# 8-wide attentions of a four-layer block: softmax division moved from the probabilities to the outputs

## The chip, the cores and the metric

The kernel runs on one core of a Trainium2 chip. The metric is the device time of one execution in microseconds. Before the change three runs took 3652.41, 3653.56 and 3655.22 us; the median is 3653.56 us.

## The reference

The program computes four layers one after the other on x of shape (16, 256, 128), float32: each adds an attention and a feed-forward part of the normalised x to x. The change touches the attentions of the first two layers, which have 16 heads of width 8:

```python
# layer 0 (layer 1 has biases, its own rope, and no mask)
q, k, v = heads(x @ Wq.T), heads(x @ Wk.T), heads(x @ Wv.T)     # (b, 16, 256, 8)
q, k = rope(q), rope(k)
scores = einsum('bhqd,bhkd->bhqk', q, k) * SCALE + causal_mask
attn = softmax(scores, axis=-1)
out = einsum('bhqk,bhkd->bhqd', attn, v)
return out.transpose(0, 2, 1, 3).reshape(b, n, 128) @ Wo.T + bo
```

## The kernel before

`program` normalises x (`norm_tiles`), then calls `prepare8` (line 274: turned and rotated weights) and `attention8` (line 319) for layer 0, with the int8 feed-forward of that layer (`Int8`) interleaved ahead of its loop; then it normalises again and calls `attention8` for layer 1. Everything else of the program (the ternary feed-forward, chunked attention, routed experts, slot experts, iterated attention) is outside of the change.

There is no planner: each engine has a program of its own, written out by hand as a loop, and engines meet through counting semaphores (`c.steps`). `attention8` works in B = 16 batches of 256 tokens. A batch is eight pairs of heads (PB = 8), so that p runs over 128 pairs, and a step j = p % 8. The steps of a pair:

- PE, `scores(p)` (line 380): two blocks of 128 queries for each of two heads, 32 rows of the array each, into PSUM banks 0 to 3, alternating; in layer 0 the causal mask is added by four bf16 matmuls. It waits for the exps of pair p-2, and at j = 0 for `laid`, the batch's queries and keys in place.
- DVE, `maxima` (line 488): a row maximum for each head over 128x512, negated.
- ACT, `exps` (line 562): two exps of 128x256 a head, which also accumulate the row sums into `rsum` (the accumulator is read out by an instruction of its own).
- DVE, `invert` (line 496): the reciprocal of the row sums. POOL, `norm` (line 609): probabilities times reciprocal, 128x512 a head.
- PE, `turn` (line 402), two pairs later: four transposes a head. ACT `move_even` (line 573) and DVE `move_odd` (line 502) copy them to SBUF.
- PE, `weigh` (line 412), after every second pair: sixteen matmuls for four heads, with the values as stationary operand, 32 columns a head. Within the 32 rows of a head r = h % 4 the eight values of head h stand at column 8 * (h // 4), zeros elsewhere (`lay_v`, line 475), so that the four groups of a batch accumulate in one PSUM tile O of 128x256. The order of the features is then a permuted one, for which `prepare8` permutes Wo by `perm`.
- Once a batch: ACT `copy_out` (line 579), PE `through_wo` (line 370), DVE `add` (line 508).

The queries and keys of a batch are prepared beside this: PE `project(b, j)` (line 351; j = 0 the queries, 1 the keys; `w[k]` and the rotated `w[k + "r"]`), DVE `rope_turn` (line 456), POOL `rotate` (line 603), DVE `hi_lo` (line 467: a rounded part and the rest), then SP (line 630) writes both parts to DRAM (`spilled`, line 640) and, after both have landed there, reads them back in another layout (`spread`, line 651; two DMAs of 256 KB). ACT `lay` (line 556) casts the landed 128x1024 into `q` or `k` and signals `laid`. All of SP's DMAs are in one queue in program order: batch by batch, queries, then keys. The loop has the keys of batch b+1 projected at step 0 of batch b and the queries of batch b+2 at step 6; `lay` of batch b+1 stands at steps 2 and 5 on ACT.

Of the kernel before, what the change touches and what calls it, by code (L numbers as in the profile page):

```python
# [16 lines left out]
P = 128  # L17
# [26 lines left out]
def const_columns():  # L44
# [9 lines left out]
    f = np.arange(P)  # L54
    head, d = f // HD8, f % HD8
    perm = np.zeros((P, P))
    perm[f, 32 * (head % 4) + HD8 * (head // 4) + d] = 1.0
    c["perm"] = perm
# [196 lines left out]
class Tiles8:  # L255


    def __init__(self, nc, sb):
# [8 lines left out]
        self.nm, self.rsum, self.rinv = (sb(f"a8_{k}", [P, 4, 2, TB]) for k in ("nm", "rsum", "rinv"))  # L267
# [3 lines left out]
        self.wo = [sb(f"a8_wo{i}", [P, D]) for i in range(2)]  # L271


def prepare8(c, t, w0, w1, bias1, perm):
# [4 lines left out]
    made, kept, zeroed = c.steps("w_made", 2), c.steps("w_kept", 2), c.steps("v_zeroed", 2)  # L279
# [3 lines left out]
    def pe_program():  # L283
# [7 lines left out]
        for n, k in enumerate("qk"):  # L291
            pe.matmul(c.banks[6][:, n * D:(n + 1) * D], t.tmp[:, n, :], c.turn, start=True, stop=True)
            pe.matmul(c.banks[6][:, 2 * D + n:2 * D + n + 1], c.turn, bias1[k], start=True, stop=True)
        pe.matmul(c.banks[7][:, 0:D], perm, t.w0[:, 3, :], start=True, stop=True)
        pe.matmul(c.banks[7][:, D:2 * D], perm, w1["o"], start=True, stop=True).then_inc(made.sem, 1)

    def act_program():
# [6 lines left out]
        act.copy(t.br1[:, :], c.banks[6][:, 2 * D:2 * D + 2])  # L304
        for i in range(2):
            ins = act.copy(t.wo[i][:, :], c.banks[7][:, i * D:(i + 1) * D])
        ins.then_inc(kept.sem, 1)
# [8 lines left out]
    return kept.all(), zeroed.all()  # L316


def attention8(c, x, xnT, tiles, ready, w, wo, rope, bias, causal, beside=None):
    nc = c.nc  # L320
    pe, act, dve, pool, sp = nc.tensor, nc.scalar, nc.vector, nc.gpsimd, nc.sync
    O, M = c.banks[6][:, 0:N], c.banks[7]
# [6 lines left out]
    t1, t2, rot, Pr, PTs, oT = tiles.t1, tiles.t2, tiles.rot, tiles.Pr, tiles.PTs, tiles.oT  # L329
    nm, rsum, rinv = tiles.nm, tiles.rsum, tiles.rinv  # L330
# [9 lines left out]
    scored, weighed = c.steps("scored", NP), c.steps("weighed", NP // 2)  # L340
    maxed, exped, inverted, normed, turned = (c.steps(k, 2 * NP) for k in ("maxed", "exped", "inverted", "normed", "turned"))
    even, odd = c.steps("even_moved", NP), c.steps("odd_moved", NP)
    out_moved, through, added = c.steps("out_moved", B), c.steps("through_wo", B), c.steps("added", B)

    def pe_program():
# [24 lines left out]
        def through_wo(b):  # L370
            if b + 2 < B:
                pe.wait_ge(*v_ready(TB * (b + 3) - 1))
            else:
                pe.wait_ge(*added(b - 1))
            pe.wait_ge(*out_moved(b))
            for t in range(TB):
                mm = pe.matmul(M[:, t * P:(t + 1) * P], oT[b % 2][:, t * P:(t + 1) * P], wo, start=True, stop=True)
# [24 lines left out]
        def turn(p, e):  # L402
            pe.wait_ge(*normed(2 * p + e))
# [8 lines left out]
        def weigh(i):  # L412
            b, j = divmod(i, PB // 2)
            if j == 0:
                pe.wait_ge(*v_ready(TB * b + TB - 1))
                if b:
                    pe.wait_ge(*out_moved(b - 1))
            pe.wait_ge(*even(2 * i + 1))
            pe.wait_ge(*odd(2 * i + 1))
            for kt in range(TB):  # L420
                for r in range(4):
                    h, p = 4 * j + r, 2 * i + r // 2
                    mm = pe.matmul(O[ROW * r:ROW * (r + 1), :], vz[b % 2][:, kt, h * ROW:(h + 1) * ROW],
                                   PTs[p % 4][:, r % 2, kt, :], start=(j == 0 and kt == 0), stop=(j == 3 and kt == TB - 1),
                                   skip_group_check=True)
            mm.then_inc(weighed.sem, 1)

        for j in range(steps):
# [4 lines left out]
            elif j == 3:  # L433
                project(1, 0)
            if beside:
                beside.pe_step(j)
        for p in range(NP + 7):
# [8 lines left out]
            if j == 0 and b + 1 < B:  # L446
                project(b + 1, 1)
            elif j == 4 and b + 1 < B:
                project_v(b + 1)
            elif j == 5 and b:  # L450
                through_wo(b - 1)
            elif j == 6 and b + 2 < B:
                project(b + 2, 0)

    def dve_program():
# [19 lines left out]
        def lay_v(b, t):  # L475
# [3 lines left out]

            width = H8 * ROW  # L480
# [2009 lines left out]
```

## Time and profile before

| | |
|---|---|
| median of three runs | 3653.56 us |
| profiled execution | 3651.16 us |
| its span, first to last instruction | 3649.9 us |
| PE busy | 3228.7 us, 88% of the span |
| DVE busy | 2619.7 us, 72% |
| ACT busy | 2495.7 us, 68% |
| POOL busy | 2294.5 us, 63% |
| mean granted TensorE clock | 0.955 |
| first attention's loop | 84 to 468 us |
| second attention's loop | 517 to 898 us |

Busy times are sums over instructions of one profiled execution. A busy PE is not a PE at its peak, as matmuls are pipelined. Two engines can overlap, so that none needs to be full where the work is bound by waits; the views of waits and of instructions in order of time tell which wait ends last. PEld is the load of stationary operands, which overlaps PE.

### The profile page before, as it was taken

How to read it: one execution, taken by the hardware profiler on the slowest of the kernel's cores; microseconds unless marked ns; L12 is line 12 of the kernel's file. 1: busy time of each engine (PE TensorE's matmuls, PEld its weight loads, DVE VectorE, ACT ScalarE, POOL GpSimd, SP SyncE). 2: the span in 40 equal slices, each digit the busy share in tenths (PEclk: the TensorE clock that was granted, in tenths of full speed). 3: DMA queues.
4: the chain of work that ended last, by engine and by line, in shares of the span. 5: the costliest groups of instructions: out<-in, count | busy, mean ns of one | idle time of the engine just before them, and what ended most of it. 6: DMA issues, size and time to landing. Idle time of an engine off the chain costs nothing.

```text
span 3649.9 us, 74432 instructions
## 1 busy us (share of the span) xinstructions
PE 3228.7 (88%) x24511; PEld 2336.4 (64%) x24511; DVE 2619.7 (72%) x5856; ACT 2495.7 (68%) x8041; POOL 2294.5 (63%) x2126
## 2 busy tenths in 40 slices
PE   4999958887773999699999799999999999999997
PEld 3666635555562888566756577677677767777775
DVE  6888868887367656644434678887777887778776
ACT  3888948887332555552533588888888888888885
POOL 4777747776121666330210688888888888888885
PEclk9999969998886999799999899999999999999999
DMA  4122112221000000300000000000000000000000
GB/s 137 62 71 71 54 38 70 69 71 36 1 1 0 1 1 1 99 13 1 1 1 1 12 2 2 1 2 2 2 2 2 2 2 2 2 2 1 2 2 24
DMA packets 54907, 78.41 MB, mean 21 GB/s; under 512 B 5952, under 2 KB 43648, under 8 KB 54272
## 3 DMA queue, kind: packets, MB, share of 16 engines
q1 hardware_dynamic: 54528, 73.65, 6.4%
q8 instruction: 202, 3.31, 0.4%
q14 instruction: 177, 1.45, 0.1%
HBM read 54.76 MB, written 18.87 MB: 20 GB/s over the span
## 4 chain that ended last, share of the span: by engine, by line
PE 43%; POOL 5%; ACT 4%; DVE 3%; issue 3%; DVEq 0%; ACTq 0%; POOLq 0%
PE psum L1918 8%; PE psum L1933 7%; PE psum L1908 7%; PE psum L1956 4%; POOL attn_p L2275 3%; PE psum L1405 3%; ACT attn_p L2030 3%; PE psum L1865 2%; POOL attn_qf L2269 2%; PE psum L1330 2%; PE psum L1416 2%; PE psum L1477 1%; PE psum L1496 1%; PE psum L1310 1%; DVE attn_nm L2150 1%
## 5 line engine op out<-in xcount | busy, mean ns | idle before, releaser
L2030 ACT ACTIVATE attn_p<-psum,attn_nm 128x256 f32<-128x256 f32 x1536 | 707.9, 477 | 253.1 <-DVE attn_nm L2150 248.6
L2275 POOL TENSOR_TENSOR attn_p<-attn_p,attn_rinv 128x512 f32<-128x512 f32 x768 | 782.6, 1040 | 133.0 <-DVE attn_rinv L2157 133.0
L612 POOL TENSOR_TENSOR sb_a_p<-sb_a_p,sb_a_rinv 128x512 f32<-128x512 f32 x512 | 529.1, 1043 | 195.6 <-DVE sb_a_rinv L500 193.9
L569 ACT ACTIVATE sb_a_p<-psum,sb_a_nm 128x256 f32<-128x256 f32 x1024 | 479.3, 506 | 75.9 <-DVE sb_a_nm L493 74.3
L2150 DVE TENSOR_REDUCE attn_nm<-psum 128x2 f32<-128x512 f32 x768 | 491.0, 680 | 20.1 <-PE psum L1908 19.9
L1933 PE MATMUL psum<-attn_pt,attn_v 128*64 128x256 f32 x3072 | 416.3, 391 | 32.4 <-DVE attn_ql L2169 28.6
L1918 PE MATMUL psum<-sb_kept,attn_p 128*128 128x128 f32 x3072 | 426.7, 280 | 8.2 <-POOL attn_p L2275 8.1
L1918 PEld LDWEIGHTS psum<-sb_kept,attn_p 128*128 128x128 f32 x3072 | 328.3, 140 | 163.5 <-issue 93.5
L408 PE MATMUL psum<-sb_kept,sb_a_p 128*128 128x128 f32 x2048 | 306.7, 284 | 79.2 <-DVE sb_a_pt L506 57.3
L493 DVE TENSOR_REDUCE sb_a_nm<-psum 128x2 f32<-128x512 f32 x512 | 343.5, 674 | 21.3 <-PE psum L398 11.5
L2030 ACT ACTIVATION_READ_ACCUMULATOR attn_p<-psum,attn_nm 128x1 f32 x1536 | 319.3, 208 | 0.0
L2163 DVE COPY attn_pt<-psum 128x512 f32<-128x512 f32 x384 | 262.6, 684 | 70.2 <-PE psum L1918 66.8
L1933 PEld LDWEIGHTS psum<-attn_pt,attn_v 128*64 128x64 f32 x3072 | 192.8, 136 | 180.3 <-issue 57.6
L408 PEld LDWEIGHTS psum<-sb_kept,sb_a_p 128*128 128x128 f32 x2048 | 221.8, 143 | 133.1 <-POOL sb_a_p L612 109.1
L1908 PE MATMUL psum<-attn_kh,attn_qh 64*128 64x256 f32 x1536 | 256.3, 330 | 1.4 <-DVE attn_ql L2127 1.4
L1167 POOL TENSOR_TENSOR moe_hh_low<-moe_h,moe_hh_high 128x512 fp32r<-128x512 f32 x136 | 176.0, 1294 | 121.0 <-ACT moe_hh_high L1194 120.4
L2038 ACT COPY attn_pt<-psum 128x512 f32<-128x512 f32 x384 | 239.4, 623 | 5.9 <-PE psum L1918 5.9
L569 ACT ACTIVATION_READ_ACCUMULATOR sb_a_p<-psum,sb_a_nm 128x1 f32 x1024 | 242.1, 237 | 0.0
L2157 DVE RECIPROCAL attn_rinv<-attn_rsum 128x4 f32<-128x4 f32 x384 | 67.7, 176 | 218.8 <-ACT attn_p L2030 215.1
L1908 PE MATMUL psum<-attn_kl,attn_qh 64*128 64x256 f32 x1536 | 216.3, 278 | 0.0
L1908 PE MATMUL psum<-attn_kh,attn_ql 64*128 64x256 f32 x1536 | 215.2, 277 | 0.0
L1381 POOL TENSOR_TENSOR slotmoe_scratch<-slotmoe_scratch,slotmoe_zi 128x512 f32<-128x512 f32 x64 | 66.5, 1039 | 220.6 <-DVE slotmoe_zi L1370 220.6
(400 smaller groups left out, 8014.2 us busy)
## 6 DMA issues: line engine op xcount, KB each, us to landing
sb_a_spread<-a_spilled SPq DMA_DIRECT2D x128, 256.0 KB, 3.1
a_spilled<-sb_a_part_hi SPq DMA_DIRECT2D x64, 128.0 KB
a_spilled<-sb_a_part_lo SPq DMA_DIRECT2D x64, 128.0 KB
sb_x<-in_L_attn_x SPq DMA_DIRECT2D x4, 512.0 KB, 6.2
sb_wg<-in_L_ffn_Wg SPq DMA_DIRECT2D x1, 2048.0 KB, 10.8
sb_wu<-in_L_ffn_Wu SPq DMA_DIRECT2D x1, 2048.0 KB, 15.6
out<-sb_x SPq DMA_DIRECT2D x4, 512.0 KB, 3.3
sb_table<-in_const SPq DMA_DIRECT2D x1, 1562.0 KB, 7.7
```

The lines of the kernel that those rows point to most:

```text
L408: mm = pe.transpose(PT(e)[:, kt * N + t * P:kt * N + (t + 1) * P], Pr[:, p % 3, e, t, kt * P:(kt + 1) * P], c.ident)
L493: dve.tensor_reduce(nm[:, p % 4, e, :], S(p, e).rearrange("p (t n) -> p t n", t=TB), AX.X, ALU.max, negate=True).then_inc(maxed.sem, 1)
L569: ins = act.activation(Pr[:, p % 3, e, t, :], S(p, e)[:, t * N:(t + 1) * N], ACT.Exp, bias=nm[:, p % 4, e, t:t + 1], accum_out=rsum[:, p % ...
L612: pool.tensor_tensor(P3, P3, spread(rinv[:, p % 4, e, :], N), ALU.mult).then_inc(normed.sem, 1)
L1908: mm = pe.matmul(S(p, e)[:, t * N:(t + 1) * N], a_[n][half(e), hp, t * P:(t + 1) * P], b_[u % 2][half(e), hp, :], start=(n_ == 0), stop=(n ...
L1918: mm = pe.transpose(PT(e)[:, kt * N + t * P:kt * N + (t + 1) * P], Pr[p % 3][:, e, t, kt * P:(kt + 1) * P], c.ident)
L1933: mm = pe.matmul(O[half(e), :], V[u % 2][:, kt, h * HD3:(h + 1) * HD3], PTs[p % 2][:, e, kt, :], start=(kt == 0), stop=(kt == TB - 1))
L2030: ins = act.activation(Pr[p % 3][:, e, t, :], S(p, e)[:, t * N:(t + 1) * N], ACT.Exp, bias=nm[:, p % 4, e, t:t + 1], accum_out=rsum[:, p % ...
L2038: act.copy(PTs[p % 2][:, 0, :, :], PT(0).rearrange("p (k n) -> p k n", k=TB)).then_inc(even.sem, 1)
L2150: dve.tensor_reduce(nm[:, p % 4, e, :], S(p, e).rearrange("p (t n) -> p t n", t=TB), AX.X, ALU.max, negate=True).then_inc(maxed.sem, 1)
L2163: dve.tensor_copy(PTs[p % 2][:, 1, :, :], PT(1).rearrange("p (k n) -> p k n", k=TB)).then_inc(odd.sem, 1)
L2275: pool.tensor_tensor(P3, P3, spread(rinv[:, p % 4, e, :], N), ALU.mult).then_inc(normed.sem, 1)
```

## The change

The probabilities stay unnormalised. The value block of a head in `vz` now holds its eight values in columns 0 to 7 and a one in column 8 (filled once by POOL), so that the row sum of the exps comes out of `weigh` as a ninth row beside the head's outputs. The groups of four heads don't accumulate in one tile any more: after each `weigh`, ACT copies the 128x256 to SBUF (`copy_sums`), PE turns it back by two transposes into the other half of the same bank (`turn_back`), and DVE takes the reciprocal of the sums and multiplies the outputs by it into `o` (`settle`). Each `weigh` waits for the `settle` ahead of it. Once a batch PE transposes `o` (`turn_out`), and `copy_out` and `through_wo` follow as before, with Wo in its natural order; `perm` and its products are gone. The reads of the accumulator, `invert` and `norm` are gone. `lay` moves from ACT to POOL, whose loop is now rotate, rotate, lay, lay for each batch. The projections of both queries and keys of batch b+1 now stand in batch b, at steps 0 and 2, their rotation at the same steps and `hi_lo` at steps 1 and 3.

```diff
-        self.nm, self.rsum, self.rinv = (sb(f"a8_{k}", [P, 4, 2, TB]) for k in ("nm", "rsum", "rinv"))
+        self.nm, self.rinv = sb("a8_nm", [P, 4, 2, TB]), sb("a8_rinv", [P, TB, 4])
+        self.sums = [sb(f"a8_sums{i}", [P, N]) for i in range(2)]
+        self.o = [sb(f"a8_o{i}", [P, TB, D]) for i in range(2)]
...
-            pool.memset(v[:, :, :], 0.0).then_inc(zeroed.sem, 1)
+            c.pool_own(pool.memset(v[:, :, :], 0.0))
+            pool.memset(v[:, :, HD8::ROW8], 1.0).then_inc(filled.sem, 1)
...
-        def through_wo(b):
+        def turn_out(b):
             if b + 2 < B:
                 pe.wait_ge(*v_ready(TB * (b + 3) - 1))
             else:
                 pe.wait_ge(*added(b - 1))
+            pe.wait_ge(*settled((b + 1) * PB // 2 - 1))
+            for t in range(TB):
+                mm = pe.transpose(M[:, t * P:(t + 1) * P], o[b % 2][:, t, :], c.ident)
+            mm.then_inc(out_turned.sem, 1)
...
         def turn(p, e):
-            pe.wait_ge(*normed(2 * p + e))
+            pe.wait_ge(*exped(2 * p + e))
...
-                if b:
-                    pe.wait_ge(*out_moved(b - 1))
+            if i:
+                pe.wait_ge(*settled(i - 1))
...
+        def turn_back(i):
+            pe.wait_ge(*summed(i))
+            for t in range(TB):
+                mm = pe.transpose(OT[:, t * P:(t + 1) * P], sums[i % 2][:, t * P:(t + 1) * P], c.ident)
+            mm.then_inc(backed.sem, 1)
...
-            elif j == 3:
-                project(1, 0)
...
-            if j == 0 and b + 1 < B:
-                project(b + 1, 1)
+            if p % 2 == 0 and 6 <= p < NP + 6:
+                turn_back((p - 6) // 2)
+            if j in (0, 2) and b + 1 < B:
+                project(b + 1, j // 2)
             elif j == 4 and b + 1 < B:
                 project_v(b + 1)
             elif j == 5 and b:
+                turn_out(b - 1)
+            elif j == 6 and b:
                 through_wo(b - 1)
-            elif j == 6 and b + 2 < B:
-                project(b + 2, 0)
...
+        def settle(i):
+
+            b, j = divmod(i, PB // 2)
+            dve.wait_ge(*backed(i))
+            if b >= 2:
+                dve.wait_ge(*out_turned(b - 2))
+            src = OT.rearrange("p (t r c) -> p t r c", t=TB, c=ROW)
+            c.dve_own(dve.reciprocal(rinv[:, :, :], src[:, :, :, HD8]))
+            out = o[b % 2][:, :, j * ROW:(j + 1) * ROW].rearrange("p t (r d) -> p t r d", d=HD8)
+            dve.tensor_tensor(out, src[:, :, :, 0:HD8], rinv[:, :, :].unsqueeze(3).to_broadcast((P, TB, 4, HD8)),
+                              ALU.mult).then_inc(settled.sem, 1)
...
-        for p in range(NP + 7):
+        for p in range(NP + 8):
             b, j = divmod(p, PB)
+            if p % 2 and 7 <= p < NP + 7:
+                settle((p - 7) // 2)
+            if j == 7 and b:
+                add(b - 1)
             if p < NP:
                 maxima(p, 0)
-            if 1 <= p < NP + 1:
-                invert(p - 1, 1)
-            if p < NP:
                 maxima(p, 1)
             if 2 <= p < NP + 2:
                 move_odd(p - 2)
-            if p < NP:
-                invert(p, 0)
             if b + 1 < B:
-                if j == 0:
-                    rope_turn(b + 1, 1)
-                elif j == 1:
-                    hi_lo(b + 1, 1)
+                if j in (0, 2):
+                    rope_turn(b + 1, j // 2)
+                elif j in (1, 3):
+                    hi_lo(b + 1, j // 2)
                 elif j == 4:
                     lay_v(b + 1, 0)
                     lay_v(b + 1, 1)
-            if b + 2 < B:
-                if j == 6:
-                    rope_turn(b + 2, 0)
-                elif j == 7:
-                    hi_lo(b + 2, 0)
-            if j == 5 and b:
-                add(b - 1)
...
-                                     bias=nm[:, p % 4, e, t:t + 1], accum_out=rsum[:, p % 4, e, t:t + 1])
+                                     bias=nm[:, p % 4, e, t:t + 1])
...
+        def copy_sums(i):
+            act.wait_ge(*weighed(i))
+            if i >= 2:
+                act.wait_ge(*backed(i - 2))
+            act.copy(sums[i % 2][:, :], O).then_inc(summed.sem, 1)
...
-            if b + 1 < B and j in (2, 5):
-                lay(b + 1, j // 3)
...
+        def lay(b, j):
+            pool.wait_ge(*landed[j](32 * (b + 1) - 1))
+            if b >= 2:
+                pool.wait_ge(*scored((b - 1) * PB - 1))
+            pool.tensor_copy((q, ks)[j][b % 2][:, :, :], spreads[j][:, :, :]).then_inc(laid.sem, 1)
...
+        for b in range(1, B):
+            for j in range(2):
+                rotate(b, j)
+            for j in range(2):
+                lay(b, j)
```

## Rows read from the trace of the kernel before

**Rows 1.** Busy time by stage (us, instructions), then granted clock, DMA share, GB/s

```profile
core 0: us, PE busy (x) PEld busy (x) DVE busy (x) ACT busy (x) POOL busy (x), PEclk, DMA share, GB/s
84.00:468.00 384.00, 350.03 (x3312) 244.69 (x3312) 331.57 (x803) 335.88 (x1199) 285.83 (x288) 1.00 0.19 62
517.00:898.00 381.00, 328.25 (x2800) 216.88 (x2800) 331.12 (x803) 335.80 (x1199) 283.15 (x285) 0.94 0.20 63
```

**Rows 2.** Groups of both attentions: line, engine, tiles, count | busy us, mean ns | idle before

```profile
L612 POOL TENSOR_TENSOR sb_a_p<-sb_a_p,sb_a_rinv 128x512 f32<-128x512 f32 x512 | 529.1, 1043 | 195.6 <-DVE sb_a_rinv L500 193.9
...
L473 DVE TENSOR_TENSOR sb_a_part_lo<-sb_a_rot,sb_a_part_hi 128x256 fp32r<-128x256 f32 x64 | 68.9, 1077 | 2.2
```

**Rows 3.** Waits of the first attention: who waited for whom, us, times, longest

```profile
POOL sb_a_p L612 <- DVE sb_a_rinv L500: 93.1, 144, 2.3
PEld psum L408 <- POOL sb_a_p L612: 37.9, 53, 1.5
```

**Rows 4.** In order of time: scores of batches 0 and 15, last adds

```profile
84.02 0.79 PE L392 MATMUL psum<-sb_a_k,sb_a_q 32*128 32x256 f32 x4 [3.33 <-ACT sb_a_k L560]
...
440.86 0.50 PE L392 MATMUL psum<-sb_a_k,sb_a_q 32*128 32x256 f32 x4
...
467.34 0.42 DVE L511 TENSOR_TENSOR sb_x<-sb_x,psum 128x256 f32<-128x256 f32 x1 [2.51 <-PE psum L377]
...
517.24 0.80 PE L392 MATMUL psum<-sb_a_k,sb_a_q 32*128 32x256 f32 x4 [10.70 <-ACT sb_a_k L560]
...
871.16 0.50 PE L392 MATMUL psum<-sb_a_k,sb_a_q 32*128 32x256 f32 x4
...
897.34 0.42 DVE L511 TENSOR_TENSOR sb_x<-sb_x,psum 128x256 f32<-128x256 f32 x1 [2.51 <-PE psum L377]
```

**Rows 5.** A cast of 128x1024 on POOL in a later layer (ns, start us)

```profile
L1782 POOL CAST sb_whi_q<-sb_se x1: 1039/1039/1039, 1617.9 to 1617.9; 128x1024 fp32r<-128x1024 f32 x1
```

**Rows 6.** PE in order of time, first attention, without waits: start us, us

```profile
246.39 1.04 PE L408 MATMUL psum<-sb_kept,sb_a_p 128*128 128x128 f32 x8
247.27 0.60 PE L359 MATMUL psum<-sb_xnT,sb_a_w 128*128 128x256 f32 x2
...
248.23 0.50 PE L392 MATMUL psum<-sb_a_k,sb_a_q 32*128 32x256 f32 x4
...
249.00 1.04 PE L408 MATMUL psum<-sb_kept,sb_a_p 128*128 128x128 f32 x8
249.98 1.07 PE L423 MATMUL psum<-sb_a_pt,sb_a_v 128*32 128x256 f32 x16
```

**Rows 7.** DVE in order of time at the start of the second attention

```profile
500.63 0.42 DVE L473 TENSOR_TENSOR sb_a_part_lo<-sb_a_rot,sb_a_part_hi 128x256 fp32r<-128x256 f32 x1
...
518.07 1.29 DVE L493 TENSOR_REDUCE sb_a_nm<-psum 128x2 f32<-128x512 f32 x2 [7.33 <-PE psum L392]
```

**Rows 8.** The first trips of the second attention, SP's queue and ACT's cast

```profile
501.15 0.56 SPq L640 DMA_DIRECT2D a_spilled<-sb_a_part_hi  x1
...
505.91 1.22 SPq L651 DMA_DIRECT2D sb_a_spread<-a_spilled  x2
507.17 0.56 SPq L640 DMA_DIRECT2D a_spilled<-sb_a_part_hi  x1
...
512.54 1.15 SPq L651 DMA_DIRECT2D sb_a_spread<-a_spilled  x2
...
516.14 1.04 ACT L560 CAST sb_a_k<-sb_a_spread 128x1024 fp32r<-128x1024 f32 x1 [5.10 <-DMA sb_a_spread<-a_spilled]
```

**Rows 9.** SP's queue, the keys' trip of a steady batch

```profile
115.65 0.57 SPq L640 DMA_DIRECT2D a_spilled<-sb_a_part_hi  x1
...
121.78 1.15 SPq L651 DMA_DIRECT2D sb_a_spread<-a_spilled  x2
```

**Rows 10.** A stop of PE, and busy time in stretches of the second attention

```profile
643.45 0.94 PE L408 MATMUL psum<-sb_kept,sb_a_p 128*128 128x128 f32 x4 [1.55 <-DVE sb_a_pt L506]
...
644.00:647.00 3.00, 3.00 (x23) 1.19 (x22) 1.35 (x3) 2.48 (x8) 1.49 (x2) 0.50 0.23 80
...
684.00:708.00 24.00, 19.71 (x177) 13.08 (x176) 21.03 (x52) 21.23 (x75) 17.81 (x18) 1.00 0.21 68
```

More of the change, by code:

```diff
@@ L270, in __init__, with prepare8 @@
         self.tmp, self.br1 = sb("a8_tmp", [P, 2, D]), sb("a8_br1", [P, 2])
-        self.wo = [sb(f"a8_wo{i}", [P, D]) for i in range(2)]
-def prepare8(c, t, w0, w1, bias1, perm):
+def prepare8(c, t, w0, w1, bias1):
     nc = c.nc
     pe, act, pool = nc.tensor, nc.scalar, nc.gpsimd
-    made, kept, zeroed = c.steps("w_made", 2), c.steps("w_kept", 2), c.steps("v_zeroed", 2)
+    made, kept, filled = c.steps("w_made", 2), c.steps("w_kept", 2), c.steps("v_filled", 2)
     pair = lambda bank, at: bank[:, at:at + 2 * D].rearrange("p (k d) -> p k d", d=D)
@@ L292, in pe_program @@
             pe.matmul(c.banks[6][:, n * D:(n + 1) * D], t.tmp[:, n, :], c.turn, start=True, stop=True)
-            pe.matmul(c.banks[6][:, 2 * D + n:2 * D + n + 1], c.turn, bias1[k], start=True, stop=True)
-        pe.matmul(c.banks[7][:, 0:D], perm, t.w0[:, 3, :], start=True, stop=True)
-        pe.matmul(c.banks[7][:, D:2 * D], perm, w1["o"], start=True, stop=True).then_inc(made.sem, 1)
+            mm = pe.matmul(c.banks[6][:, 2 * D + n:2 * D + n + 1], c.turn, bias1[k], start=True, stop=True)
+        mm.then_inc(made.sem, 1)
     def act_program():
@@ L315, in prepare8, with attention8 @@
     pool_program()
-    return kept.all(), zeroed.all()
-def attention8(c, x, xnT, tiles, ready, w, wo, rope, bias, causal, beside=None):
+    return kept.all(), filled.all()
+def attention8(c, x, xnT, tiles, ready, w, rope, bias, causal, beside=None):
     nc = c.nc
     pe, act, dve, pool, sp = nc.tensor, nc.scalar, nc.vector, nc.gpsimd, nc.sync
-    O, M = c.banks[6][:, 0:N], c.banks[7]
+    O, OT, M = c.banks[6][:, 0:N], c.banks[6][:, N:2 * N], c.banks[7]
     S = lambda p, e: c.banks[2 * (p % 2) + e]
@@ L338, in attention8 @@
     v_ready = c.steps("v_parted", TB * B)
[L340 to L341 removed]
+    scored = c.steps("scored", NP)
+    weighed, summed, backed, settled = (c.steps(k, NP // 2) for k in ("weighed", "summed", "backed", "settled"))
+    maxed, exped, turned = (c.steps(k, 2 * NP) for k in ("maxed", "exped", "turned"))
     even, odd = c.steps("even_moved", NP), c.steps("odd_moved", NP)
[L343 removed]
+    out_turned, out_moved, through, added = (c.steps(k, B) for k in ("out_turned", "out_moved", "through_wo", "added"))
     def pe_program():
@@ L587, in act_program @@
                 beside.act_step(j)
-        for j in range(2):
-            lay(0, j)
-        for p in range(NP + 5):
+        for p in range(NP + 7):
             b, j = divmod(p, PB)
-            if b and j == 4:
+            if p % 2 == 0 and 6 <= p < NP + 6:
+                copy_sums((p - 6) // 2)
+            if j == 6 and b:
                 copy_out(b - 1)
```

82 lines of the change are left out of this document (23 added, 59 removed).

## Prediction

> **What bounds the kernel now.** The change touches only the two 8-wide attentions, so I read busy times over their two stretches first. The first runs from 84 to 468 us with PE 350, DVE 332, ACT 336 and POOL 286 us busy; the second from 517 to 898 us with 328, 331, 336 and 283 us [rows 1]. No engine is full: about a tenth of each stretch goes to waits. The list of waits names them. POOL, which only normalises (1.04 us an instruction, 512 of them [rows 2]), waits 93.1 us for the reciprocals, and PE's weight loads of the transposes wait 37.9 us for POOL, in the first stretch alone [rows 3]. So the ring of exp, row sum, reciprocal, normalising and transpose costs latency; the change takes exactly that ring apart.
>
> For the arithmetic I use the start of one batch to the start of the next. Scores of batch 0 start at 84.02 and of batch 15 at 440.86: 23.79 us a batch; in the second attention 517.24 to 871.16: 23.59 [rows 4]. What follows the start of batch 15 takes 26.9 us (to the end of the last add, 467.34 + 0.42) and 26.6 us [rows 4].
>
> **Parts with one answer.** PE's transposes wait for the exps, no longer for POOL. ACT loses 32 reads of the accumulator a batch; it also loses two `lay` casts a batch, and gains four copies of 128x256. It is far from a bound afterwards. POOL loses 16 multiplications a batch (16.6 us) and takes the two casts: an equal cast on POOL took 1.04 us [rows 5]. DVE loses 16 reciprocals and gains four `settle` a batch. The trace has no `settle` (reciprocal of 128x8, a wait for it, a product of 128x64, both from PSUM); it lies between two small DVE instructions, 0.3 us, and one large one and a wait, 0.8; I take 0.4, as both tiles are small. Dropping the two products with `perm` and their copies saves well under 1 us at 44 us, beside the integer branch: nothing.
>
> **PE's own load.** From one stretch without waits [rows 6]: scores with masks 0.77 (248.23 to 249.00), eight transposes 0.88 (246.39 to 247.27), or 0.98 before `weigh`, `weigh` 1.0, a projection of four matmuls 0.96. New are `turn_back`, two transposes per four heads (2/8 of 0.88, with a wait 0.28), and `turn_out`, the same once a batch. A batch of the first attention then sums to 8 x (0.77 + 0.88) + 4 x 1.1 + 4 x 0.28 + 2 x 0.96 + 0.6 (values) + 0.9 (`turn_out`, `through_wo`) = 22.1 us; the second has no masks (0.34 a pair): 19.4. DVE: two maxima and one copy a pair at 0.60 each (two maxima take 1.29 us with the tail of the last [rows 7]), 14.4 a batch, and about 5.4 for the rotation, parting, values, adding and `settle`: 19.8.
> Parting (`hi_lo`) changes too. Its subtraction takes 1.08 us in the mean of 64 [rows 2] but 0.42 us where POOL was idle [rows 7]; POOL will be idle in both, so 0.42. (The Trainium skill, SBUF — State Buffer, on engine ports, says a DVE instruction with two SBUF inputs and a GpSimd instruction that reads SBUF exclude each other for a whole instruction; by that the next cast on POOL would add up to its own length if it fell on a parting. By the order below it does not, and the trace's two durations agree with the rule.)
> By the engines alone, a batch would therefore come down by 1.5 us and by nearly 4 us.
>
> **The step that is moved.** The queries of batch b+1 are now projected at step 0 of batch b and the keys at step 2; before, the queries went two steps ahead of the batch before, at step 6, and the keys at step 0. So both trips through DRAM now lie between the start of batch b and that of b+1, and both are on one SP queue. SP does: spill q, wait, spread q, spill k, wait, spread k. The keys' spill cannot be issued ahead of the queries' spread. With T the start of a batch:
> - T to the spill of q. PE: scores 0.77, transposes 0.88, `turn_back` 0.28, projection 0.96 plus its tail, at T+3.05. DVE rotates (0.67), settles (0.4), does two maxima and a copy of step 1 (1.8), parts (0.74): T+6.65, and 0.1 to SP. Sum 6.7; second attention 6.55 (no masks, slower rotation with bias).
> - Spill q to spread q: 4.76 (501.15 to 505.91 [rows 8]). Spread q to spill k: 1.26. The keys are parted two steps later, about T+12.4, when SP comes free at T+12.7.
> - Spill k to spread k: 5.37 in the quiet start of the second attention [rows 8], 6.13 in the first steady batch [rows 9]; behind a spread of q in all 28 steady batches it lies between 5.1 and 6.2. I take 5.65.
> - Spread k to landed 3.60 (512.54 to 516.14 [rows 8]), the cast on POOL 1.04 [rows 5], signals 0.15. Then T+23.2 (first) and T+23.0 (second).
> This is longer than PE's 22.1 and much longer than the second attention's 19.8. It becomes what ends last: the scores wait for `laid`, and behind them in PE's queue stand the transposes, `weigh` and the next projection, so nothing of batch b+1's own trip can start early. The new wait feeds itself.
> (The Trainium skill, DMA: Bandwidth & Descriptors, gives some 2.0 us of fixed cost for a DMA; with the issue time an estimate from that is about 3.2 us for a spill. The row says 4.76 and decides; by the page the trip would not bind, which is the second rival.)
>
> **The clock.** In the second attention PE would then stand still for about 23.0 - 19.8 = 3.2 us a batch. Before, a stop of 1.55 us ahead of 643.45 was followed by three microseconds at granted clock 0.50, that is 1.2 GHz, though PE was 100% busy in them [rows 10]; over the stretch the clock was 0.94, against 1.00 in the first attention [rows 1]. So I expect each stop to be followed by slow work, and it would fall on the head of the trip (scores, transposes, projection: 2.6 us of PE work, double at half clock). At most that adds 2.6 us a batch, at least nothing; I take 1.6, as the slow stretch should begin in part before T, as at 643, and last 3 us: 24.6 us a batch. In the first attention the stop is only about 1 us and the clock should hold; allowing for small waits of PE I take 23.3.
>
> **The sum**, against the profiled execution of 3651.16 us (span 3649.9 and 1.3 around it):
> - first attention: start 1.9 earlier (two casts of 1 us no longer between the integer branch and the scores, 84.02 against about 82.1): -1.9. Fifteen batches at 23.3 for 23.79: -7.4. The last has no trip to wait for; its pairs lose the waits for POOL and gain 1.4 us of turning back and out, of which I keep 0.7 (between 0 and 1.4); the new tail (copy sums, turn back, settle twice in a row, turn out, copy, `wo`) against the old one adds 1.6: +2.3. Together -7.0.
> - second attention: start the same (q and k travel there as before, POOL's cast as long as ACT's). Fifteen at 24.6 for 23.59: +15.2; +1 as the first batch starts at half clock. The last: without masks PE has room, so its pairs become cheaper by 1.5 (between 0 and the 3.8 that the engines' load gives), tail +1.6: 0. Together +16.2.
> 3651.2 - 7.0 + 16.2 = 3660.4 us. The median of the runs shown is 3653.56, 2.4 above the profiled execution, so I forecast 3662 us.
>
> **The rivals.**
> 1. The clock does not pay: PE stands, but its slow microseconds fall where nothing waits, or the clock holds. Then both attentions run at the trip's pace, 23.3 and 23.0: -7.0 - 8.9 = -16, 3638 us. For it: from 684 to 708 us, in a whole batch of the second attention, the clock held at 1.00 with the same work [rows 10]. Against: the stop doubles in length. 0.20.
> 2. The trip does not bind: its hops are shorter than the rows say, and the engines set the pace, with waits of their own 22.2 and 20.6 us a batch: -1.9 - 23.9 + 2.3 - 44.9 = -68, 3585 us. For it: the busy sums. Against: every hop was read from the same DMAs with the same sizes. 0.13.
> 3. Slower throughout: the trip is longer than summed, in one place: parting waits at its head (`settle` at 0.8 instead of 0.4, the subtraction at 1.08 instead of 0.42 because POOL is not idle), +1.0 us in each of 30 batches over my sum, and the first attention's stop then reaches 2 us and loses the clock too: 3662 + 30 = 3692 us. It turns from faster to slower once the trip is 0.5 us longer in the first attention, and 0.6 in the second. 0.20.
> 4. The change does not do what it says (PE still waits elsewhere for as long as it did for POOL, so that the batch stays at 23.7): 3656 us. 0.05.
> The forecast has 0.42, and its own range is 3650 to 3676.
>
> **How the numbers follow.** A measurement of this kernel tells about 0.2% from no change, 7.3 us: faster is under 3646.3, slower over 3660.9. The forecast splits at its middle: 0.02 faster, 0.17 same, 0.23 slower. Faster: rivals 1 (but for 0.02) and 2, 0.31, and that 0.02, 0.33; same: 0.17 + 0.05 + 0.02 of rival 1 = 0.24; slower: 0.23 + 0.20 = 0.43. The range goes from rival 1's low side, 3626, to 3692, the point of rival 3; it leaves out rival 2 and the upper half of rival 3 beyond, about 0.2.
>
> **What would show it.** Scores' first matmul of each batch (the line of `scores`) waiting for POOL's cast of the keys, 15 times in each attention, 1 us each in the first and 3 to 4 in the second; on SP, spill k right behind spread q; the batch at 23.3 and 24.6 us; granted clock under 0.9 in the second attention, falling before or at each batch's start. POOL under a third of its busy time; ACT and DVE falling, the subtraction at 0.42. I am wrong if PE waits for nothing of `laid`, if the trip from spill q to spread k takes clearly less than 11.7 us, or if the clock stays at 1.00 after stops of 3 us.

## The result, and the profile after the change

The kernel with the change takes 3663.16 us (median of 20 runs, 3652.67 to 3669.7); the kernel before, run beside it, 3652.57 us (20 runs, 3649.3 to 3656.27). The ratio is 1.0028, 95% interval 1.0022 to 1.0035: slower by 10.6 us. The profiled execution of the changed kernel took 3667.24 us with a span of 3665.9, 16.0 more than the span of before, so it lies a little above the median.

An engine's work fell, yet the time did not. Busy time by stage, the page's view of before in [rows 1], here of the changed kernel (us and instructions; then granted clock, DMA share, GB/s), with three single batches of the first attention under it:

```profile
84.00:468.00 384.00, 361.30 (x3464) 269.08 (x3463) 310.13 (x675) 284.23 (x719) 55.94 (x63) 0.97 0.19 63
517.00:912.00 395.00, 346.83 (x2956) 247.92 (x2956) 310.93 (x675) 284.75 (x718) 54.10 (x61) 0.91 0.19 62
...
129.13:154.36 25.23, 21.91 (x219) 16.40 (x219) 19.56 (x43) 17.80 (x45) 3.54 (x4) 1.00 0.19 64
178.65:201.49 22.84, 21.91 (x218) 16.41 (x218) 19.56 (x43) 17.85 (x46) 3.54 (x4) 1.00 0.22 71
225.13:249.69 24.56, 23.59 (x220) 17.87 (x220) 19.66 (x43) 17.80 (x45) 3.54 (x4) 0.93 0.20 66
```

POOL went from 286 to 56 us, ACT from 336 to 284, DVE from 332 to 310; PE rose from 350 to 361. A batch holds 21.91 us of PE work at a clock of 1.00, and takes 22.8 to 25.4. What PE waits for is in the list of waits, first attention and then second (who waited for whom: us, times, longest):

```profile
PEld psum L392 <- POOL sb_a_k L608: 28.3, 15, 3.8
PEld psum L392 <- ACT sb_a_p L560: 21.3, 55, 0.7
PE psum L392 <- POOL sb_a_k L608: 21.1, 15, 3.3
```

```profile
PEld psum L392 <- POOL sb_a_k L608: 61.5, 16, 14.0
PE psum L392 <- POOL sb_a_k L608: 54.0, 16, 13.7
```

The two waits of [rows 3] are gone. In their place the scores (L392) wait for POOL's cast of the keys, once in every batch, 15 times and 16 (one of those 16, the 14 us, is the start of the second attention). The row with ACT is the weight loads' ordinary short wait for exponentials, 0.4 us in the mean; e1 below, which is faster, has it too. In order of time, two whole batches: one of the first attention and one of the second.

```profile
106.23 0.50 PE L392 MATMUL psum<-sb_a_k,sb_a_q 32*128 32x256 f32 x4 [1.60 <-POOL sb_a_k L608]
...
112.78 0.56 SPq L633 DMA_DIRECT2D a_spilled<-sb_a_part_hi  x1
...
117.58 1.22 SPq L644 DMA_DIRECT2D sb_a_spread<-a_spilled  x2
...
118.84 0.57 SPq L633 DMA_DIRECT2D a_spilled<-sb_a_part_hi  x1
...
124.33 1.15 SPq L644 DMA_DIRECT2D sb_a_spread<-a_spilled  x2
128.03 1.04 POOL L608 CAST sb_a_k<-sb_a_spread 128x1024 fp32r<-128x1024 f32 x1 [5.24 <-DMA sb_a_spread<-a_spilled]
...
129.13 0.50 PE L392 MATMUL psum<-sb_a_k,sb_a_q 32*128 32x256 f32 x4 [0.98 <-POOL sb_a_k L608]
```

```profile
542.83 0.50 PE L392 MATMUL psum<-sb_a_k,sb_a_q 32*128 32x256 f32 x4 [3.20 <-POOL sb_a_k L608]
...
550.88 0.55 SPq L633 DMA_DIRECT2D a_spilled<-sb_a_part_hi  x1
...
555.83 1.22 SPq L644 DMA_DIRECT2D sb_a_spread<-a_spilled  x2
555.83 0.42 DVE L478 TENSOR_TENSOR sb_a_part_lo<-sb_a_rot,sb_a_part_hi 128x256 fp32r<-128x256 f32 x1
557.09 0.56 SPq L633 DMA_DIRECT2D a_spilled<-sb_a_part_hi  x1
...
562.47 1.15 SPq L644 DMA_DIRECT2D sb_a_spread<-a_spilled  x2
566.17 1.04 POOL L608 CAST sb_a_k<-sb_a_spread 128x1024 fp32r<-128x1024 f32 x1 [5.47 <-DMA sb_a_spread<-a_spilled]
567.27 0.79 PE L392 MATMUL psum<-sb_a_k,sb_a_q 32*128 32x256 f32 x4 [2.33 <-POOL sb_a_k L608]
```

The first batch is the trip and nothing else: 6.55 + 4.80 + 1.26 + 5.49 + 3.70 + 1.10 = 22.90 us from scores to scores. These terms are: the head (from the scores to the queries' spill), the queries' spill, the issue of their spread, the keys' spill, their spread to its landing, and the cast with its signals. The second batch has a head of 8.05, 24.44 in all: after the stop of 3.20 us PE ran at half speed. Where the clock stayed up in the second attention (batches from 592.20 and 838.37) the head is 6.38. Two stretches of three microseconds, the first one behind a short stop (the scores at 106.23), the second one behind that of 3.20:

```profile
107.00:110.00 3.00, 3.00 (x27) 2.46 (x25) 2.72 (x6) 2.06 (x5) 0.00 (x0) 1.00 0.00 0
...
543.00:546.00 3.00, 3.00 (x16) 2.78 (x17) 1.98 (x3) 1.63 (x5) 0.00 (x0) 0.56 0.00 0
```

PE is full in both, with 27 instructions against 16 (counted as in all these rows), at a granted clock of 1.00 and 0.56. Read in half-microseconds, the clock of the changed kernel falls to 1.2 GHz five times in the first attention (before: never) and, behind the start of the second, after 13 of its 15 stops at a batch's head (before: 9 times).

Against the kernel before [rows 4], by stage:

| | before | after | difference |
|---|---|---|---|
| first scores | 84.02 | 83.16 | -0.9 |
| first attention, a batch | 23.79 | 23.91 | 15 x 0.12 = +1.8 |
| its last batch and tail | 26.9 | 29.5 | +2.6 |
| second attention, a batch | 23.59 | 24.40 | 15 x 0.81 = +12.1 |
| its last batch and tail | 26.6 | 28.8 | +2.2 |

(After: scores of the first and the last batch 83.16 to 441.78 and 520.89 to 886.95, last adds ending at 471.31 and 915.76.) With 0.1 more between the attentions that is +18.0 at 916 us; the layers behind, which the change does not touch, give back 2.0: +16.0 in the span.

### The profile page after: what moved, and what is told of

Read it like the earlier page. It is cut to its first block, busy times and chain, and to the rows that moved or that the text cites. A ratio compares the mean times of both kernels' runs of the same rounds, so it can differ in the third digit from the quotient of the medians.

```text
span 3665.9 us, 73136 instructions
## 1 busy us (share of the span) xinstructions
PE 3255.1 (89%) x24827; PEld 2389.3 (65%) x24827; DVE 2576.0 (70%) x5600; ACT 2393.1 (65%) x7079; POOL 1837.7 (50%) x1680
## 4 chain that ended last, share of the span: by engine, by line
PE 43%; POOL 5%; ACT 4%; DVE 3%; issue 3%; DVEq 0%; ACTq 0%; POOLq 0%
PE psum L1911 8%; PE psum L1926 7%; PE psum L1901 7%; PE psum L1949 4%; POOL attn_p L2268 3%; PE psum L1398 3%; ACT attn_p L2023 3%; PE psum L1858 2%; POOL attn_qf L2262 2%; PE psum L1323 2%; PE psum L1409 2%; PE psum L1489 1%; PE psum L1470 1%; PE psum L1303 1%; DVE attn_nm L2143 1%
## 5 line engine op out<-in xcount | busy, mean ns | idle before, releaser
L560 ACT ACTIVATE sb_a_p<-psum,sb_a_nm 128x256 f32<-128x256 f32 x1024 | 403.8, 485 | 46.3 <-DVE sb_a_nm L496 43.3
L496 DVE TENSOR_REDUCE sb_a_nm<-psum 128x2 f32<-128x512 f32 x512 | 328.5, 683 | 132.2 <-PE psum L398 67.3
L408 PE MATMUL psum<-sb_kept,sb_a_p 128*128 128x128 f32 x2048 | 291.6, 287 | 0.7 <-DVE sb_a_pt L515 0.4
L568 ACT COPY sb_a_pt<-psum 128x512 f32<-128x512 f32 x256 | 152.0, 594 | 176.7 <-PE psum L408 175.6
L408 PEld LDWEIGHTS psum<-sb_kept,sb_a_p 128*128 128x128 f32 x2048 | 231.5, 146 | 25.3 <-issue 7.8
L392 PE MATMUL psum<-sb_a_k,sb_a_q 32*128 32x256 f32 x1024 | 135.6, 345 | 79.2 <-POOL sb_a_k L608 75.2
L602 POOL TENSOR_TENSOR sb_a_rot<-sb_a_t 128x256 f32<-128x256 f32 x64 | 46.7, 729 | 302.1 <-DVE sb_a_t L469 233.5
## 6 DMA issues: line engine op xcount, KB each, us to landing
sb_wg<-in_L_ffn_Wg SPq DMA_DIRECT2D x1, 2048.0 KB, 10.6
```

What stands on the lines that cost most here:

```text
L408: mm = pe.transpose(PT(e)[:, kt * N + t * P:kt * N + (t + 1) * P], Pr[:, p % 3, e, t, kt * P:(kt + 1) * P], c.ident)
L496: dve.tensor_reduce(nm[:, p % 4, e, :], S(p, e).rearrange("p (t n) -> p t n", t=TB), AX.X, ALU.max, negate=True).then_inc(maxed.sem, 1)
L560: ins = act.activation(Pr[:, p % 3, e, t, :], S(p, e)[:, t * N:(t + 1) * N], ACT.Exp, bias=nm[:, p % 4, e, t:t + 1])
```

## The experiments

Theory T: the two trips through DRAM, one behind the other on SP's one queue and both within one batch, set the batch; the clock adds to it where PE stops. Rival R: the engines' own work, or the new chain from exponentials to settled outputs, sets it. Rival C: the clock's falls are the cause and not the trip. All kernels below ran beside runs of the kernel before; a batch's length is read from DVE's adds of consecutive batches or from the scores.

### The queries a batch earlier, the rest of the change kept (e1)

```diff
 # pe_program, after the steps of pair p
-            if j in (0, 2) and b + 1 < B:
-                project(b + 1, j // 2)
+            if j == 0 and b + 1 < B:
+                project(b + 1, 1)
+            elif j == 2 and b + 2 < B:
+                project(b + 2, 0)
 # dve_program: rope_turn(b + 1, 1) at 0, hi_lo(b + 1, 1) at 1, rope_turn(b + 2, 0) at 2, hi_lo(b + 2, 0) at 3
 # pool_program: rotate(b, 1), rotate(b + 1, 0), lay(b, 0), lay(b, 1); the waits on M follow the new order
```

> The changed kernel, with the queries prepared a batch earlier, as before the change: projected at step 2 for the batch after next, the keys at step 0 for the next one; the two casts stay on POOL. Nothing else differs. If the two trips through DRAM, one behind the other, set the batches (23.9 us a batch in the first attention, 24.4 in the second), the keys' trip alone now starts at step 0 and is laid by T + 17 or so; the scores never wait for the cast, PE never stops for it, and the clock holds: 22.2 to 22.8 us a batch in the first attention, 20.4 to 21.2 in the second, the whole near 3590 us (3575 to 3605), 0.983 of the kernel before. If the batches are set by the engines' own work, or by a longer chain from exponentials to settled outputs, the periods stay at 23.9 and 24.4 and the time near 3663 us. If only the clock's falls cost, and they come from elsewhere than this wait, they stay, and so does the time.

Measured: 3570.78 us (3568.53 to 3571.68), ratio 0.9773, interval 0.9757 to 0.9789. Every steady batch takes 21.84 us in the first attention and 20.37 in the second, to a hundredth; behind the start of each attention, the list of waits has none of L392 for the cast. Twelve batches of the first attention of e1, busy time and clock:

```profile
121.65:383.73 262.08, 262.08 (x2619) 196.84 (x2617) 234.78 (x517) 213.13 (x541) 41.68 (x48) 1.00 0.23 74
```

PE is busy for 262.08 of 262.08 us. So R is out as an account of 23.9 and 24.4: the engines can do 21.84 and 20.37, and in the first attention nothing but PE sets that. In the second PE is busy 200.82 of 203.68 us (ten batches from 526.48); e8 shows that ScalarE has a part in that pace too. The order of preparation alone costs 92 us (3663.2 against 3570.8). The forecast of T, 3590, was too slow by 19: the engines' pace was put some 0.4 to 0.7 us a batch too high.

### The order of preparation alone, in the kernel before (e2)

```diff
 # the kernel before; pe_program
-            if j == 0 and b + 1 < B:
-                project(b + 1, 1)
+            if j in (0, 2) and b + 1 < B:
+                project(b + 1, j // 2)
...
-            elif j == 6 and b + 2 < B:
-                project(b + 2, 0)
 # dve_program, pool_program: the same places
 # act_program
-            if b + 1 < B and j in (2, 5):
-                lay(b + 1, j // 3)
+            if b + 1 < B and j in (6, 7):
+                lay(b + 1, j - 6)
```

> The kernel before, with one part of the change alone: the queries of the next batch are projected at step 0 and its keys at step 2, and ScalarE casts them at steps 6 and 7 rather than 2 and 5. Normalised probabilities, the division on POOL and everything else stay. If the order of preparation costs what the trips through DRAM take, this is slower than the kernel before: the keys land near T + 21.9, and the cast is queued on ScalarE behind the exponentials of step 7, so 24 to 25 us a batch against 23.8 and 23.6, the whole 3665 to 3695 us. If the old pace of 23.7 came from the division on POOL alone and the order is covered by it, the time is that of the kernel before, within 0.2% of 3653 us.

Measured: 3748.8 us (3744.99 to 3750.36), ratio 1.0259, interval 1.0242 to 1.0276; steady batches of 27.1 and 27.3 us. The sign was right, the size was not: 3.3 to 3.7 us a batch instead of 0.2 to 1.4. One batch of e2, scores at 379.46 to scores at 406.49:

```profile
388.18 0.55 SPq L627 DMA_DIRECT2D a_spilled<-sb_a_part_hi  x1
...
393.18 1.22 SPq L638 DMA_DIRECT2D sb_a_spread<-a_spilled  x2
394.44 0.55 SPq L627 DMA_DIRECT2D a_spilled<-sb_a_part_hi  x1
...
400.17 1.15 SPq L638 DMA_DIRECT2D sb_a_spread<-a_spilled  x2
...
405.34 1.10 ACT L549 CAST sb_a_k<-sb_a_spread 128x1024 fp32r<-128x1024 f32 x1
...
406.49 0.50 PE L392 MATMUL psum<-sb_a_k,sb_a_q 32*128 32x256 f32 x4 [3.38 <-ACT sb_a_k L549]
```

Three microseconds in that batch's head, and the first three of the next one's:

```profile
381.00:384.00 3.00, 3.00 (x13) 1.88 (x12) 2.31 (x7) 2.29 (x9) 2.08 (x2) 0.50 0.00 0
406.50:409.50 3.00, 3.00 (x24) 2.36 (x24) 2.00 (x5) 1.59 (x6) 1.04 (x1) 1.00 0.00 0
```

The head is 8.72 us instead of 6.55. Two things make it so. The clock fell inside it (0.50 from 381 to 384 us); the head of the next batch, from 406.49, where the clock held behind a stop just as long, takes 7.30, and that batch 25.61 in all. So the clock costs some 1.4 us a batch, and the expectation had nothing for it. The other 0.7 go with the parting's subtraction, which takes 1113 ns (x57) and not 425: here POOL still normalises beside it. And the cast starts 5.17 us after the issue of the spread, not 3.70, because four exponentials stand ahead of it on ScalarE. So the same order costs about as much in the kernel before (95 us) as in the changed one (92), and the rest of the change brings 83 us without the order (before to e1) and 86 with it (e2 to after). The two parts add up, and nearly cancel.

### Both spills ahead of both spreads (e5)

```diff
 # sp_program
         for b in range(B):
             for j in range(2):
                 # the spill of j
+            for j in range(2):
+                box = tiles.spilled[j]
                 sp.wait_ge(*away[j](32 * (b + 1) - 1))
                 # the spread of j
```

> The changed kernel with the order of its one queue altered: both spills of a batch, then both spreads, in place of spill q, spread q, spill k, spread k. In the trace of the changed kernel the keys are ready at 556.25 us and their spill starts at 557.09, behind the spread of the queries that has been issued from 555.83 on. If the trips set the batch, the keys' spill starts 0.8 us sooner and so does everything behind it: 32 x 0.8, some 25 us less, near 3638 us (3625 to 3650), and the clock falls in as many batches as before, or fewer. If the trips do not set the batch, the time stays at 3663 us.

Measured: 3609.13 us (3607.5 to 3611.28), ratio 0.9882, interval 0.9865 to 0.9898: 54 us under the changed kernel, twice the forecast. A batch of the second attention of e5, from scores to scores:

```profile
622.78 0.50 PE L392 MATMUL psum<-sb_a_k,sb_a_q 32*128 32x256 f32 x4 [1.44 <-POOL sb_a_k L608]
...
629.16 0.57 SPq L633 DMA_DIRECT2D a_spilled<-sb_a_part_hi  x1
...
634.57 0.50 SPq L633 DMA_DIRECT2D a_spilled<-sb_a_part_hi  x1
...
645.04 0.50 PE L392 MATMUL psum<-sb_a_k,sb_a_q 32*128 32x256 f32 x4 [1.81 <-POOL sb_a_k L608]
```

It takes 22.26 us. In the changed kernel the batch from 542.83 to 567.27 above has 6.21 us between the spills, here 5.41, and 10.47 from the keys' spill to the next scores instead of 10.18, so between these two only some 0.5 us are won on the queue. The rest of the difference between them is the head: 6.38 instead of 8.05, since the stop before it was 1.44 us instead of 3.20 and the clock did not fall. Averaged over all fifteen batches of each attention the queue's part is larger: from the queries' spill to the next scores the changed kernel takes 16.8 us in both, e5 15.8 and 15.7, and the heads give another 0.6 and 0.9. The clock falls behind none of the fifteen stops of the first attention (five in the changed kernel) and behind five of the second (13). Batches: 22.38 and 22.50 us; the first scores start 3.1 us sooner. T holds; what my forecast left out is that a shorter trip also takes the clock's part away.

### Filler where PE stands still (e4)

```diff
         def scores(p):
             b, j = divmod(p, PB)
-            if j == 0:
-                pe.wait_ge(*laid(2 * b + 1))
...
             if p >= 2:
                 pe.wait_ge(*exped(2 * (p - 2) + 1))
+            if j == 0 and b:
+                for _ in range(8 if causal else 24):
+                    pe.matmul(S(p, 0)[:, 0:N], c.mask400, c.future0, start=True, stop=True, skip_group_check=True)
+            if j == 0:
+                pe.wait_ge(*laid(2 * b + 1))
```

> The changed kernel with filler on TensorE ahead of the wait for the cast keys at the start of a batch: 8 matmuls of the mask in the first attention (0.85 us at 0.107 each) and 24 in the second (2.6 us), into a bank that the scores overwrite. They add work only where TensorE stands still. If the falls of the clock after those stops are what lifts the period over the trip, the clock holds near 1.0 through both attentions and the periods fall to that of the trip, 22.9 and 23.0 us: 16 x 1.0 and 16 x 1.4 less, some 35 us, near 3627 us (3615 to 3645). If the trip alone sets the period and the low clock is hidden, the time stays at 3663 us or grows by a little (to 3675).

Measured: 3644.52 us (3641.49 to 3651.01), ratio 0.9978, interval 0.9969 to 0.9988: 19 us under the changed kernel, for more work on PE. The clock falls once in the first attention and not at all in the second after its start. The filler fills the stop:

```profile
603.82 1.07 PE L426 MATMUL psum<-sb_a_pt,sb_a_v 128*32 128x256 f32 x16
604.82 2.79 PE L386 MATMUL psum<-sb_fut,sb_mask 128*128 128x256 bf16 x24
607.54 0.50 PE L395 MATMUL psum<-sb_a_k,sb_a_q 32*128 32x256 f32 x4
```

That batch began at 584.45: 23.09 us at a clock of 1.00, and seven of the fifteen of this attention take between 22.69 and 23.13. The means are 23.60 and 23.45 against 23.91 and 24.40, 15 x 0.31 + 15 x 0.95 = 19 us. That is about the least that the clock cost: the heads alone, 7.15 and 7.61 us on average in the changed kernel and 6.76 and 6.33 here, differ by 25 us, of which e4's own trips, longer behind the head, gave some back. In four batches of the second attention the filler also ended later than the cast (by 0.06 to 0.6 us). C is out: without falls no batch is shorter than 22.69, where the engines can do 21.84 or 20.37. The forecast of 35 us was too high for another reason as well: some batches are long without a fall, in both kernels. In the changed kernel the batch from 129.13 to 154.36 takes 25.23 at a clock of 1.00:

```profile
148.01 1.15 SPq L644 DMA_DIRECT2D sb_a_spread<-a_spilled  x2
153.26 1.04 POOL L608 CAST sb_a_k<-sb_a_spread 128x1024 fp32r<-128x1024 f32 x1 [7.10 <-DMA sb_a_spread<-a_spilled]
154.36 0.79 PE L392 MATMUL psum<-sb_a_k,sb_a_q 32*128 32x256 f32 x4 [3.32 <-POOL sb_a_k L608]
```

The spread took 5.25 us to land, where it takes about 3.7 in most of the thirty batches; two more took 5.50 and 5.27 us. The long stop that comes with each (3.32, 2.81 and 3.92 us) brought a fall of the clock as well. In e4 four of the thirty took 4.77 to 5.75 us.

### Keys one step earlier (e6), and that with the spills first (e7)

```diff
 # e6: pe_program
-            if j in (0, 2) and b + 1 < B:
-                project(b + 1, j // 2)
+            if j < 2 and b + 1 < B:
+                project(b + 1, j)
 # dve_program: rope_turn of q and k at 0 and 1, hi_lo at 1 and 2
 # e7: this, and the sp_program of e5
```

> The changed kernel with the keys prepared one step earlier, at step 1 rather than 2, and the queue's order left as it is. In the changed kernel the keys' spill starts 1.26 us after the spread of the queries has begun to be issued (555.83 and 557.09 us), though the keys are ready at 556.25: the spread stands ahead of it. With the keys ready some 2.7 us sooner, the spread still stands ahead, since it waits for the queries' spill. If the one queue with its two trips in a row sets the batch, nothing moves: 23.9 and 24.4 us a batch, 3663 us (3650 to 3668, the clock's falls can shift). If it is the work on the keys up to their spill that sets it, 32 x 2.7 us go, down to the pace of the engines: near 3580 us.

> The changed kernel with both: keys prepared at step 1, and both spills ahead of both spreads. The two trips then overlap: the keys' spill at about T + 9, its spread at T + 14, landed at T + 18, cast by T + 19.2. That is below the engines' own pace as the kernel with queries prepared early showed it (21.84 and 20.37 us a batch), so if only the trip held the changed kernel back, this one runs at that pace too: 3570 to 3585 us. If the early queries of that kernel helped in another way (less work of VectorE or of TensorE crowded into one part of the batch), this one stays above it, near 3600 us.

Measured: e6 3659.53 us (3651.53 to 3662.33), ratio 1.0012, interval 1.0002 to 1.0022; e7 3577.07 us (3575.25 to 3577.56), ratio 0.979, interval 0.9773 to 0.9806. Keys that are ready 2.7 us sooner gain next to nothing alone, since the queue does not take them:

```profile
573.85 1.22 SPq L644 DMA_DIRECT2D sb_a_spread<-a_spilled  x2
575.11 0.56 SPq L633 DMA_DIRECT2D a_spilled<-sb_a_part_hi  x1
```

1.26 us again in e6, between the issue of the queries' spread and that of the keys' spill. With the queue's order altered too, both together are worth 86 us, 32 more than that order alone (e5). e7's batches take 22.28 and 20.70; it stays 6 us behind e1, with PE busy 265.30 of 267.36 us in twelve batches where e1 has 262.08 of 262.08. Which of its small waits does that was not separated. In e6's first attention the clock held after 113.5 us, and its batches from 133.22 to 436.44 take 23.32 on average: the trip's pace with the clock at 1.00, as the prediction had it.

### The casts back on ScalarE (e8), the first casts behind the adds (e9)

```diff
 # e8 = e1, with lay() in act_program after the exponentials
+            if b + 1 < B and j in (2, 5):
+                lay(b + 1, j // 3)
 # e9 = e1, pool_program
-            elif j in (4, 5):
-                lay(0, j - 4)
             if beside:
                 beside.pool_step(j)
+            if j in (4, 5):
+                lay(0, j - 4)
```

> The kernel with queries prepared early, and its two casts a batch moved back from POOL to ScalarE, after the exponentials of steps 2 and 5 as in the kernel before. If POOL's cast of 1.04 us (also 1.04 to 1.06 on ScalarE) matters only by its place in the trip, nothing binds there now: ScalarE is busy 292 of 384 us in the first attention, so 16 x 2.1 us more fit in, and the time is 3571 us (3565 to 3580). If exponentials bind the pace of 21.84 and 20.37, each cast delays them by 1.04 us: up to 2.1 a batch, near 3638 us.

> The kernel with queries prepared early, with the first two casts on POOL put behind that step's scaling and adding of the int8 rows rather than ahead. In the changed kernel the first cast of the keys stands ahead of them on POOL, ScalarE waits 4.40 us for POOL's add at 76.75, and the first scores start at 83.16; with queries prepared early they start at 82.24. If that wait is what delays the start, they start near 81.3 and everything ends 1 us sooner, 3570 us; as a time that is within what can be told from no change, so the start of the first scores in the trace decides. If the adds themselves set the start, it stays at 82.2.

Measured: e8 3583.75 us (3582.91 to 3584.36), ratio 0.9807, interval 0.9791 to 0.9824; 13 us behind e1. Its batches take 21.97 (+0.13) and 21.16 (+0.79): in the first attention, which PE fills, the casts fit in; in the second, ScalarE's two casts of about 1.04 us show in part. So moving them to POOL is worth 13 us, where neither expectation (nothing, or 67) fits. e9: 3569.96 us (3569.0 to 3572.12), ratio 0.9771, interval 0.9755 to 0.9787; the first scores start at 81.94 instead of 82.24, where 81.3 was expected. The casts do not leave POOL's queue by this, they move within it: the keys' cast at 74.34 now stands ahead of the next step's scaling, from 75.34. That a start without them would be 1 us sooner was not tried. e1 and e9 are equal within what can be told and are the fastest versions: 2.3% faster than the kernel before, with all of the change but its order.

## Why the prediction was right, and where only in sum

The time came to 3663.16 us for 3662 forecast, and the mechanism was the one forecast: scores waiting for the cast, each batch, behind two trips in a row. Its terms were not all right.

- **The trip.** Forecast T+23.2 in the first attention; the batch at 106.23 took 22.90. By hop, forecast and measured: to the spill 6.7 and 6.55; 4.76 and 4.80; 1.26 and 1.26; 5.65 and 5.49; 3.60 and 3.70; cast and signals 1.19 and 1.10. This batch is one of the quick ones: in e6's first attention from 133.22 us on, where the clock held and no spread landed late, the batches average 23.32, as the keys' spill takes 5.15 to 6.3 us. e1, e5 and e7 show that it binds: each shortens it in another way, and each takes the batches down. (The Trainium skill, DMA: Bandwidth & Descriptors, on fixed cost, led to an estimate of 3.2 us for a spill in the prediction; the queries' spill measured 4.75 to 5.46 us, 4.84 on average, and decides.)
- **Rival 2** was wrong as a forecast, but its price is what the kernel can do without the trip: 22.2 and 20.6 us a batch and 3585 us, against 21.84, 20.37 and 3570.78 in e1. PE's load, summed to 22.1 us, was 21.91.
- **The first attention: -7.0 forecast, +3.6 measured.** The failed step is "In the first attention the stop is only about 1 us and the clock should hold". Ten of its stops are 0.6 to 1.6 us, and the clock held after each of them; five are 1.67, 1.73, 1.78, 2.81 and 3.32 us, and it fell after all five. Two of the long ones follow slow landings of the spread (5.25 and 5.50 us for 3.7). Of the 1.0 us a batch between 22.90 and 23.91, heads slowed by the clock make 0.6, slow landings 0.2, and spills that took longer than those of the batch shown 0.2. Against the 23.3 forecast that is +9.2 us over 15 batches. Where the clock held in e6, 23.32 was measured. The start adds another 1.0: 0.9 us earlier and not 1.9.
- **The second attention: +16.2 forecast, +14.5 measured**, as 24.40 a batch for 24.6. The two steady batches whose head ran at full clock take 23.23 and 23.15 us (trip forecast: 23.0), the twelve others 24.81 on average (24.6); the first, which has nothing of an earlier batch at its head, 21.94. The clock's term of 1.6 us for such a batch was thus right in size; the head shows it, 7.98 on average in the twelve and 6.38 in the two. Its stops were forecast at 3.2 us and are 2.06 to 3.92, 2.7 on average, and the granted clock is 0.91 where under 0.9 was named as a sign. The last batch and the tail were forecast even and cost +2.2 (low clock from 888.0 to 891.5 us among it).
- **The rest** of the program, taken as unchanged, ended 2.0 us nearer. Sum: forecast +9.2 on the span (3660.4 us; with the 2.4 between profiled execution and median 3662.8, which the prediction gives as 3662), measured +16.0 in the profiled execution and +10.6 in the medians. The agreement to 1 us is thus partly luck: the first attention was 10.6 us too optimistic, the second with what follows 3.8 too pessimistic, and the profiled execution lies 4 us above the median, where that of before lay 1.4 under its own.
- **Costs of single operations** held: the exponentials lost their accumulator reads, the subtraction takes 425 ns, and `settle` 198 + 225 ns and 34 between them, 0.46 us for 0.4 forecast:

```profile
L478 DVE TENSOR_TENSOR sb_a_part_lo<-sb_a_rot,sb_a_part_hi 128x256 fp32r<-128x256 f32 x64 | 27.2, 425 | 2.2
...
L508 DVE TENSOR_TENSOR sb_a_o<-psum,sb_a_rinv 128x64 f32<-128x64 f32 x128 | 28.7, 225 | 4.4
...
L506 DVE RECIPROCAL sb_a_rinv<-psum 128x8 f32<-128x8 f32 x128 | 25.4, 198 | 6.7 <-PE psum L430 6.7
```

The same subtraction took 1077 ns in the kernel before [rows 2] and 1113 in e2, the two in which POOL normalises beside it. (The Trainium skill, SBUF — State Buffer, on engine ports, says that two-input work of DVE and SBUF reads of GpSimd exclude each other; the three kernels agree with it.)

## What to carry to other kernels

A change can hold two parts that cancel: here the arithmetic, worth 83 to 86 us, and a moved step of preparation, which costs 92 to 95. When a diff moves a step, follow everything it feeds, on every queue, from its new place to who waits for it, and compare that length with the period that the other part promises. Do not take it that the moved step is hidden because the old period was long: in the kernel before it costs 95 us (e2). Where two round trips share a queue, issue all first halves ahead of all second halves, and try the queue's order together with earlier data: e6 gave nothing and e5 54 us, but both together 86. Short waits that recur every period in front of TensorE can cost more than their length: behind stops of 2.1 to 3.9 us the slow clock took another 1.6 us of the next batch.

## What the runs showed of the hardware

- Stops of 1.67 to 1.78 us in the first attention were each followed by some 3.4 us at 1.2 GHz, and one of 1.60 was not; in e5's second attention one of 1.71 was and ones of 1.79, 1.81 and 1.86 were not, and in the changed kernel's neither were two of 2.92 and 2.06 (592.20 and 838.37 us). Length alone does not decide it. (The Trainium skill, TensorE: Matmul & The Clock Gate, on oscillation, describes a kernel that loses the clock at every tile because it waits for its DMA; these traces show it behind 13 of 15 such waits of the second attention and 5 of 15 of the first, so not every time.)
- Useless matmuls in a stop made the kernel 19 us faster (e4): the only run here in which adding work saved time.
- The same spread through the same queue landed in about 3.7 us in most batches and in 5.25 to 5.50 in three. In each of these three, one 16 KB packet of a queue that the profile calls "q8 instruction", not one of the program's transfers, ran beside it (it started 2.75 to 3.0 us after the issue and took about 0.95 us); with none of the other 27 did one start in the first 3.3 us. In e4 four of thirty landed late (4.77 to 5.75 us), each with such a packet 1.2 to 3.3 us after the issue, and one with a packet at 2.75 landed in 3.80. So the two go together, but not always, and no run tested it as a cause. A kernel whose trip is hidden does not show this: e1's batches agree to 0.01 us. The runs of the changed kernel spread over 17.0 us, those of the kernel before over 7.0, those of e1 over 3.2 (4 runs); that late landings make that spread is not shown, as e5, which waits for its trip too, spreads over 3.8 (4 runs).
